# A ring of eleven gathered tiles, an earlier token list and another order of GpSimd's transfers in the q, k, v products of a routed feed-forward

## The reference

```python
def _fff(x, nw, nb, w1, b1, w2, b2, act):
    node = jnp.zeros(x.shape[:2], dtype=jnp.int32)
    for _ in range(DEPTH):                       # DEPTH = 8, 256 leaves
        logit = jnp.einsum('bsd,bsd->bs', x, nw[node]) + nb[node]
        node = 2 * node + 1 + (logit > 0).astype(jnp.int32)
    leaf = node - NN
    h = act(jnp.einsum('bsd,bsdl->bsl', x, w1[leaf]) + b1[leaf])
    return jnp.einsum('bsl,bsld->bsd', h, w2[leaf]) + b2[leaf]
...
q = _fff(xn, q_nw, q_nb, q_w1, q_b1, q_w2, q_b2, relu)
k = _fff(xn, k_nw, k_nb, k_w1, k_b1, k_w2, k_b2, relu)
v = _fff(xn, v_nw, v_nb, v_w1, v_b1, v_w2, v_b2, relu)
att = jax.nn.softmax(jnp.einsum('bqd,bkd->bqk', q, k) / jnp.sqrt(jnp.float32(D)), axis=-1)
y = xn + jnp.einsum('bqk,bkd->bqd', att, v)
return y + _fff(y, f_nw, f_nb, f_w1, f_b1, f_w2, f_b2, gelu)
```

## Time and profile before

| | us |
|---|---|
| median of 3 runs | 1479.96 |
| lowest, highest | 1478.77, 1485.66 |
| the profiled execution | 1475.21 |
| its span in the trace | 1473.2 |
| TensorE busy in it | 1235.5 (84%) |
| VectorE busy | 883.5 (60%) |
| ScalarE busy | 582.3 (40%) |
| GpSimd busy | 446.1 (30%) |

### The profile page before, as it was taken

How to read it: one execution, slowest core, us unless ns; L and a number is a source line. 1 busy time by engine, 2 the same in 40 slices (tenths; PEclk the granted TensorE clock), 3 DMA queues, 4 the chain that set the end, 5 groups by cost and what they waited for, 6 DMA issues and landing times. The chain is left out here.

```text
span 1473.2 us, 24697 instructions
## 1 busy us (share of the span) xinstructions
PE 1235.5 (84%) x7236; PEld 899.8 (61%) x7236; DVE 883.5 (60%) x2513; ACT 582.3 (40%) x1106; POOL 446.1 (30%) x588
## 2 busy tenths in 40 slices
PE   1297999999876885897888849589999889999997
PEld 1195777777665764675667737466666555555554
DVE  7998989999613674655454457354556425444534
ACT  2124565665321233464553227144565531212110
POOL 2258344555552045443434327321121000000000
PEclk9658999999988988898989879788999889999999
DMA  9000000000001812758347316710000000000000
GB/s 277 2 2 2 1 1 1 1 1 1 0 1 23 287 55 80 247 176 279 106 124 248 124 40 126 204 15 8 9 9 8 1 1 1 14 0 14 0 15 14
DMA packets 85380, 92.70 MB, mean 63 GB/s; under 512 B 19400, under 2 KB 70090, under 8 KB 85260
## 3 DMA queue, kind: packets, MB, share of 16 engines
q1 hardware_dynamic: 72972, 66.05, 14.2%
q0 software_dynamic: 12288, 25.18, 7.1%
HBM read 76.51 MB, written 14.68 MB: 62 GB/s over the span
## 5 line engine op out<-in xcount | busy, mean ns | idle before, releaser
L3399 ACT ACTIVATE m_silu<-m_psG 128x512 f32<-128x512 f32 x48 | 28.7, 597 | 215.3 <-PE m_psU L3519 215.3
L3452 DVE TENSOR_TENSOR m_act<-m_silu,m_psU 128x512 f32<-128x512 f32 x48 | 33.0, 688 | 122.4 <-ACT m_silu L3399 107.7
L2191 PE MATMUL gq_psH<-gq_xT,gq_w 128*128 (+1 forms) x564 | 100.6, 304 | 4.3 <-ACT gq_w L1898 2.8
L2074 DVE SCALAR_TENSOR_TENSOR gq_hT<-gq_xT,unit_leaf,gq_act 128x128 f32<-128x128 f32 x141 | 49.8, 353 | 84.7 <-ACT gq_act L1906 58.5
L2191 PEld LDWEIGHTS gq_psH<-gq_xT,gq_w 128*128 128x128 f32 x564 | 80.8, 204 | 30.0 <-issue 25.9
L2201 PE MATMUL gq_psY<-leaf_w,gq_hT 128*128 (+1 forms) x282 | 90.9, 406 | 4.8 <-DVE gq_hT L2074 4.6
L3519 PE MATMUL m_psG<-m_xnT,m_gate 128*128 128x512 f32 x192 | 92.0, 602 | 2.1 <-PEq L192 2.1
L3519 PE MATMUL m_psU<-m_xnT,m_up 128*128 128x512 f32 x192 | 90.6, 594 | 0.0
L1792 POOL DMA_INDIRECT gq_x<-rows_x,gq_token_i x48 | 46.0, 958 | 118.4 <-DVE gq_tile_row L2067 62.3
L765 DVE MATCH_REPLACE8 s_product_a_rest<-a_top,s_product_a_rest 128x256 f32<-128x256 f32 x192 | 76.1, 408 | 0.3 <-issue 0.3
L205 POOL TENSOR_SCALAR m_rstd<-m_mean_var 128x4 f32<-128x4 f32 x4 | 0.9, 231 | 240.1 <-DVE m_mean_var L1297 240.1
(11 more groups left out here) (554 smaller groups left out, 3098.2 us busy)
## 6 DMA issues: line engine op xcount, KB each, us to landing
leaf_w<-in_group_w SPq DMA_DIRECT2D x128, 128.0 KB, 3.9
leaf_w<-in_group_w SPq DMA_DIRECT2D x64, 256.0 KB, 4.9
a_w<-in_L_xattn_W SPq DMA_DIRECT2D x2, 1024.0 KB, 12.0
rows_x<-token_rows SPq DMA_DIRECT2D x8, 256.0 KB, 4.8
sorted_y_q<-gq_y SPq DMA_DIRECT2D x16, 128.0 KB, 4.8
sorted_y_k<-rows_ahead SPq DMA_DIRECT2D x16, 128.0 KB, 5.0
sorted_y_v<-gq_y SPq DMA_DIRECT2D x16, 128.0 KB, 2.0
rows_f<-token_rows SPq DMA_DIRECT2D x8, 256.0 KB, 2.7
```

The costliest lines, as they stand in the source:

```text
L2074: dve.scalar_tensor_tensor(hT[n % 2][:], xT[:, DC, bass.ds(g * -P + u * P, P)], leaves.unit_leaf[:, bass.ds(g, 1)], act_h[n % 2][:], ALU.i ...
L2191: last = pe.matmul(psH[n % 2][:, 0:P], w1[n % 3][:, c, :], xT[:, c, bass.ds(g * -P + u * P, P)], start=(c == 0), stop=(c == DC - 1))
```

## The change

The ring has eleven buffers; its five new ones take 5 KB a partition, and 4 KB come back because routing's `side` and `leaf` tiles are now views of the three `w1` tiles and of `act`, made one tile. The rule of two transfers under way now counts both kinds together. The token list of q is made in items 10 to 14, not 10 to 18. GpSimd's queue gets another order.

```diff
-    RING = 6 if nf > 1 else NT
+    RING = 11 if nf > 1 else NT
...
-        self.side = [sb(f"side{n}", [P, 2, S], BF16) for n in range(2)]
-        self.leaf = [sb(f"leaf{n}", [P, 2, S], BF16) for n in range(2)]
+        self.side, self.leaf = spaces[0:2], spaces[2:4]
...
-        act_h = [sb(f"act{n}", [P, P]) for n in range(2)]
+        acts = sb("act", [P, 2, P])
+        act_h = [acts[:, n] for n in range(2)]
...
             route = Routing(core, own, tokens, leaves, places, rows, nw, xnT,
-                            (psX, psH, psY[1:3]))
+                            (psX, psH, psY[1:3]),
+                            [part[:].bitcast(BF16) for part in (*w1, acts)])
...
-                    if n >= 2:
-                        pool.wait_ge(tile_in[(n - 2) % RING], 16 * ((n - 2) // RING + 1))
+                    if len(under_way) >= 2:
+                        pool.wait_ge(*under_way[-2])
+                    under_way.append((tile_in[n % RING], 16 * (n // RING + 1)))
...
-                    if t >= 2:
-                        pool.wait_ge(seeded[t - 2], 16 * (f + 1))
+                    if len(under_way) >= 2:
+                        pool.wait_ge(*under_way[-2])
+                    under_way.append((seeded[t], 16 * (f + 1)))
...
-                    for t in range(RING):
+                    for t in range(NT):
                         gather(0, t)
-                    for t in range(NT):
                         seed(0, t)
-                    for t in range(RING, NT):
-                        gather(0, t)
                     for f in range(1, nf):
+                        for t in range(RING):
+                            gather(f, t)
                         for t in range(NT):
                             seed(f, t)
-                        for t in range(NT):
+                        for t in range(RING, NT):
                             gather(f, t)
```

More of the change, by code:

```diff
@@ L1457, with __init__ @@
     ITEMS = B + 2 * B
-    def __init__(self, core, ctx, tokens, leaves, places, rows, nw, xnT, banks):
+    def __init__(self, core, ctx, tokens, leaves, places, rows, nw, xnT, banks, spaces):
         self.core, self.tokens, self.leaves = core, tokens, leaves
@@ L1782, in _ @@
             def _(pool):
+                under_way = []
                 def gather(f, t):
@@ L2106, in _ @@
                             route.dve_take(dve, do, i - 2)
+                        if i == B + 2:
+                            starts(0, 0)
+                            starts(0, 1)
                         if i == B + 3:
-                            starts(0, 0)
+                            slots(0, 0)
+                            slots(0, 1)
                         if i == B + 4:
-                            starts(0, 1)
-                        if i == B + 5:
-                            slots(0, 0)
+                            locate(0, 0)
+                            locate(0, 1)
                         if i == B + 6:
-                            slots(0, 1)
+                            found_tokens(0)
                         if i == B + 7:
-                            locate(0, 0)
+                            steps(0, 0)
                         if i == B + 8:
-                            locate(0, 1)
-                        if i == B + 9:
-                            steps(0, 0)
+                            steps(0, 1)
                         if i == B + 10:
[L2122 to L2125, removed]
                             pack(0)
@@ L2272, in _ @@
                             route.pe_follow(pe, i - 1)
+                        if i == B + 2:
+                            count(0)
+                            rank(0)
                         if i >= 2:
                             route.pe_look_up(pe, i - 2)
-                        if i == B + 3:
-                            count(0)
-                            rank(0)
+                        if i == B + 5:
+                            find_tokens(0)
                         if i == B + 9:
-                            find_tokens(0)
-                        if i == B + 12:
                             words_of(0)
```

## The result

The changed kernel takes 1472.09 us (median, 1465.55 to 1479.6), where the kernel before, run beside it on the same chip, takes 1480.82 (1473.67 to 1488.74). The ratio is 0.9933, with a 95% interval of 0.991 to 0.9955: 9.9 us faster, between 6.7 and 13.3. Two later comparisons gave 0.9914 (0.9885 to 0.9944) and 0.9955 (0.9929 to 0.9982). The forecast was 14.7 us and 1465, in a range of 1449 to 1477: the direction is right, about two thirds of the size came.

The account below looks back on a forecast made before the run. The prediction took GpSimd's queue of indirect transfers to bound the q, k, v products. The list's 7.5 us and the order's 7.2 us made 14.7 us, from 1479.96 to 1465 us, in a range of 1449 to 1477.

Parts of the forecast that it names:

- The bound: In the q, k, v products, GpSimd's queue of 96 indirect transfers bounds, for a gain of 14.7 us; chance 0.57.
- the second rival: In the products, TensorE bounds throughout: v's last turn at 693, 33 us sooner, 1447 us; all or most of v, chance 0.15.
- The list: In routing, q's token list comes sooner: first gather at 520.6 us, a lead of 7.5 us, bounds 6 and 8.6.
- The order's 7.2 us: In GpSimd's queue, the new order takes 186.4 us for 95 intervals against 193.6, bringing 7.2 us.
- bounds for the order: Other paces beside and away from the loads in GpSimd's queue put the order's part between -1 and +17 us.
- the first rival: Contention in the load stretches: queue never rests, transfers and loads slow each other, run takes 1499 us; chance 0.06.
- the third rival: List only 5 us sooner, biases ahead of tiles 11 to 15 eat order's gain: 1475; with half the contention, 1480; chance 0.22.
- Adding the two halves: At v's last turn, the order's 7.2 us and the list's 7.5 us sum to 14.7 us.
- v's first and later tiles: In v, TensorE waits not for the first tile but ahead of tiles 11 to 15 and their biases.
- What follows that turn is unchanged: Behind v's last turn, units without turns at 0.95 us, then the next stage, which starts 15 us sooner.

Follow-up runs that it names:

- e_noseed: The changed kernel without the 32 bias transfers of k and v, so its result is not the reference's: 1442.63 us, 0.9794 of the kernel before.
- e_order: The changed kernel with the token list made as late as before (ring of eleven and new order alone): 1478.59 us, 1.0016 of the kernel before.
- e_thin: The changed kernel with loads of k's and v's weights cut to a quarter of their columns, result not the reference's: 1447.43 us, 0.9827 of the kernel before.
- e_b3: The changed kernel with GpSimd's ahead gathers cut from 16 to 12, the other four moved into the attention: 1469.36 us, 0.9978 of the kernel before.
- r_after: The changed kernel run again, unedited, in the first later comparison: 1471.73 us, 0.9914 of the kernel before.
- r_after2: The changed kernel run once more, unedited, in the second later comparison: 0.9955 of the kernel before.
- e_slide: The changed kernel with the sixteen ahead gathers held two under way one at a time, not in whole pairs: 1474.56 us, 0.997 of the kernel before.
- e_three: The changed kernel with three transfers under way instead of two in the q, k, v products: 1532.01 us, 1.0368 of the kernel before.
- e_three_seed: The changed kernel with three transfers under way in k's and v's bias transfers alone: 1469.56 us, 0.9905 of the kernel before.

## Why the prediction was right, and where its sum was not

**The bound: right.** GpSimd's queue ended last in q and v. With a third of its transfers left out (e_noseed) v's last turn is at 696.44, near the 693 that the second rival had for a TensorE bound; with all of them that rival did not come about. The Trainium skill's fit for such a transfer ("DMA: Bandwidth & Descriptors", section "Anatomy of one DMA — SWDGE (gpsimd) path"), 2.3 us for 128 KB, would have let TensorE bound. The trace does not agree: with two under way one of k's biases was issued each 2.51 us.

**The list: right.** First gather 520.85 (forecast 520.6), TensorE's waits for is_row 3.7 us (3.5), first turn 546.60 (545, so 1.6 us late). That the gather is right to 0.3 us is in part luck, as this start varies by more. That the queue covers these is shown by q's last turn, 573.30, with a wait for a transfer.

**The order's 7.2 us: wrong.** This is the term that failed. I gave 21 intervals 3.0 us and the other 74 between 1.6 and 1.72, 186.4 in sum; they took 194.4. By stretches, measured against given: q's 32 took 53.2 us for 51.2, k's first eleven tiles 20.9 for 18.9, k's biases 40.2 for 40.3, the sixteen tiles behind them 36.25 for 32.6, v's biases 36.7 for 36.5, the last four intervals 7.2 for 6.9. So two paces were mis-sized. Of the 8.0 us some 5.5 lie away from the loads: from q's tile 11 on the intervals there are 1.83 to 1.90 us and not 1.6 and 1.72. Some 2 us lie beside them: of the sixteen tiles five, not four, fell into v's load stretch, at 3.16 us and not 3.0. The prediction's bounds for the order (-1 to +17) held it at their end.

The pace away from the loads is something that the rows of before already had. A pair of transfers takes 3.0 us up to the gather of tile 10 and 3.5 from there to the end of q. Tile 11 is the first for which the queue waits not only for a transfer but also for TensorE to have turned the tile in its buffer. The changed kernel, and then e_order, which starts 5.3 us later and has the step at the same tile:

```profile
549.11 0.94 POOL L1796 DMA_INDIRECT gq_x<-rows_x,gq_token_i  x1 [0.65 <-DMA gq_x<-rows_x,gq_token_i]
...
552.11 0.95 POOL L1796 DMA_INDIRECT gq_x<-rows_x,gq_token_i  x1 [0.78 <-DMA gq_x<-rows_x,gq_token_i]
...
555.57 0.94 POOL L1796 DMA_INDIRECT gq_x<-rows_x,gq_token_i  x1 [1.27 <-PE gq_psX L2181]
```

```profile
557.49 0.95 POOL L1796 DMA_INDIRECT gq_x<-rows_x,gq_token_i  x1 [0.98 <-DMA gq_x<-rows_x,gq_token_i]
...
560.93 0.94 POOL L1796 DMA_INDIRECT gq_x<-rows_x,gq_token_i  x1 [1.19 <-PE gq_psX L2184]
```

All ten traces with the new order and two under way in q have it (median of the first ten pairs 2.98 to 3.06 us, of the next six 3.45 to 3.75). In the kernel before, with its ring of six, q's first 22 intervals took 1.54 us and its last ten, gathers into used buffers, 1.78; the prediction's 1.61 is the mean of both. The turns had long been done, so it is no wait for TensorE, and with three under way such gathers were issued each 1.25 us. Why they cost a pair 0.5 us no run shows.

Against the kernel before, the order's cost lies where the prediction had it: k's biases took 27.5 us away from the loads and take 40.2 beside them, and e_thin, with 29.4, shows that the loads' bytes make most of the difference. That is the mechanism of the first rival, too small to make the time worse. What came about is nearest to the second half of the third rival: the queue takes no less time, and the lead at its end, 6.35 us, is the list's 7.2 less 0.9, which the larger ring keeps.

**Adding the two halves: wrong at the queue.** The sum put 7.5 us for the list beside 7.2 for the order. Apart they moved the last gather by 1.7 and 0.9 us, together by 6.35. The list's lead needs the larger ring, or most of it is lost at 630 us; the ring needs the lead, or there is nothing for it to keep.

**v's first and later tiles: right.** No wait for tile 0 (678.11), 17.18 us ahead of tile 11. v's last turn moved by 7.85 us and not 14.7.

**"What follows that turn is unchanged": half wrong.** v's last turn to TensorE's DRAIN took 34.5 us before and 35.4 now. But the attention waits for all engines, and GpSimd's 16 ahead gathers and its DRAIN of 11.64 us do not follow TensorE. From the last gather to the attention it is 45.9 us before and 49.2 now, since the ahead gathers took 35.8 us and not 32.5. So of 7.85 us at the last turn, 3.0 reached the attention. e_b3 shows the mechanism: with the DRAIN out of the way the attention started as soon as SyncE's end let it.

**What stays open, and what was luck.** The attention starts 3.0 us sooner in the first trace of the changed kernel and 5.2 and 4.9 in the two later ones (762.32, 762.59); the stage behind it 2.7, 2.6 and 5.2 us. The medians say 9.9, with an interval down to 6.7. With one trace of the kernel before, 1475.21 us where its median beside it was 1480.82, I can't place the other 2 to 7 us. The direction follows from the mechanism; that the time came as near to 1465 us as 1472.09 is in part luck, since the queue gave 6.35 us of the 14.7 and the attention's start 3.0 to 5.2. What lies behind 855 us varies by itself: 622.3 us in one execution of the changed kernel and 612.3 in another. The windows 855:1000 of these two (the traces of r_after and r_after2), where the granted clock is 0.76 and 0.80:

```profile
855.00:1000.00 145.00, 109.97 (x640) 81.54 (x643) 76.81 (x191) 59.24 (x132) 60.47 (x55) 0.76 0.41 96
```

```profile
855.00:1000.00 145.00, 112.69 (x725) 82.85 (x726) 78.79 (x189) 63.71 (x137) 61.32 (x56) 0.80 0.41 96
```

## What to carry to other kernels

Where a queue with a fixed number of transfers is the bound, ask of another order which transfers it moves beside the loads: here that took back the pause which it removed. Don't take a mean pace from a stretch that holds two kinds of transfer; q's 1.61 us was 1.54 and 1.78. Ahead of "what follows is unchanged", read the end of the stage for every engine, its DRAIN among them. Here a third transfer under way paid where the other engines waited for the queue, and cost more than it brought where the queue ran ahead of them.

## What the runs showed of the hardware

- GpSimd's DRAIN grew with the indirect transfers that its block had issued: 9.02 us with 80, 11.31 with 108, 11.64 with 112, some 0.08 us each. The number is not all: behind the attention's 32 it was 4.35 to 5.2, and in this stage, with 112 but one semaphore for each ahead gather, it was 10.40 (e_slide). The other engines' take at most 0.8 us there.
- While GpSimd issued an indirect transfer each 1.25 us for 20 us or so (e_three, and k's biases in e_three_seed), VectorE and ScalarE stood for 4 to 12 us at a time and TensorE with them, at a DMA share of 0.35 in the first of these stretches. In e_three the last stop of each burst ended 4.0 to 4.4 us behind the burst's last issue. I have not settled why. In the changed kernel's window 525:545 three packets of the instruction queues were moved and in e_three's none, so late instructions are one reading; semaphores that arrive late are another, and no run here tells them apart.
- With two transfers of 128 KB under way one was issued each 1.56 us in q up to tile 10 (DMA share 0.28) and each 1.83 behind it (0.27), each 1.84 among k's biases at a share of 0.62 (e_thin) and each 2.51 at 0.86.
